# Attention scores as one plain fp32 product of q and k instead of three products of their split halves

## What is computed

```python
q = rms_norm((layernorm(x) @ Wq).reshape(b, lq, 4, 64), qn_w)
k, v = split(ctx @ Wkv);  k = rms_norm(k, kn_w)
attn = softmax(einsum('bqhd,bkhd->bhqk', q, k) / sqrt(64))
x = x + tanh(g_xattn) * (einsum('bhqk,bkhd->bqhd', attn, v) @ Wfc + fc_b)
xn = layernorm(x);  w, e = top2_softmax(xn @ Wr.T)
x = x + tanh(g_ffn) * sum_k w_k * (xn @ We[e_k])      # up to capacity 97
```

## Time and profile before

| | before |
|---|---|
| median of 3 runs | 1433.06 us |
| profiled execution | 1432.43 us |
| its span | 1430.7 us |
| TensorE, matmuls | 1396.8 us busy, 98% |
| TensorE, weight loads | 1174.7 us busy, 82% |
| VectorE | 77% busy |
| ScalarE | 65% busy |
| GpSimd | 54% busy |
| granted TensorE clock | 0.993 of full speed |

### The profile page before, as it was taken

The page is one execution under the profiler, slowest core; times in us unless marked ns, Lnnn a source line. Parts: engine busy times, 40 slices in busy tenths (PEclk is TensorE's granted clock), DMA queues, the critical chain, the costliest instruction groups (busy, mean ns, idle before and its releaser), DMA issues. The chain is left out here.

```text
span 1430.7 us, 27376 instructions
## 1 busy us (share of the span) xinstructions
PE 1396.8 (98%) x8478; PEld 1174.7 (82%) x8478; DVE 1108.2 (77%) x3146; ACT 926.7 (65%) x2600; POOL 768.8 (54%) x915
## 2 busy tenths in 40 slices
PE   5799999999999999999999999999999999999998
PEld 4688888888888888888888888888888888888876
DVE  6777878778878788878778878778778778777764
ACT  6656667666677666677666676666676666676652
POOL 3345555555555555555555555555554655554644
PEclk9899999999999999999999999999999999999999
DMA  5000000110100110100110100010101110101000
GB/s 150 20 9 28 34 35 9 35 35 28 35 19 24 35 35 27 35 15 29 35 35 28 35 9 35 35 35 28 35 9 35 35 35 28 35 9 35 16 16 23
DMA packets 29074, 43.65 MB, mean 31 GB/s; under 512 B 4672, under 2 KB 12288, under 8 KB 28928
## 3 DMA queue, kind: packets, MB, share of 16 engines
q1 hardware_dynamic: 28928, 41.90, 8.7%
HBM read 25.11 MB, written 16.78 MB: 29 GB/s over the span
## 5 line engine op out<-in xcount | busy, mean ns | idle before, releaser
L317 PE MATMUL bkM<-we,x2T 128*128 128x512 f32 x3072 | 784.7, 398 | 1.2 <-DVE acc_v L1029 1.2
L317 PEld LDWEIGHTS bkM<-we,x2T 128*128 128x128 f32 x3072 | 551.9, 188 | 125.3 <-ACT a_out L649 10.0
L649 ACT ACTIVATE a_out<-bkM,gate 128x256 f32<-128x256 f32 x512 | 215.6, 476 | 184.8 <-PE bkM L317 180.9
L1029 DVE SCALAR_TENSOR_TENSOR acc_v<-bkM,gate,acc_v 128x256 f32<-128x256 f32 x384 | 184.9, 481 | 48.0 <-PE bkM L317 32.9
L465 POOL TENSOR_TENSOR a_sum<-a_sum,a_out 128x256 f32<-128x256 f32 x256 | 188.5, 736 | 57.6 <-ACT a_out L649 21.1
L452 POOL TENSOR_TENSOR probs<-probs,p_inv 128x308 f32<-128x308 f32 x128 | 91.6, 717 | 177.1 <-DVE p_inv L922 177.1
L421 POOL TENSOR_TENSOR q_r<-q_ve,minus_half 128x16 f32<-128x16 f32 x32 | 93.1, 2911 | 112.8 <-DVE q_ve L907 112.8
L421 POOL TENSOR_TENSOR rstd<-ve,minus_half 128x4 f32<-128x4 f32 x64 | 65.3, 1020 | 159.6 <-DVE ve L822 159.4
L554 ACT ACTIVATE xn<-x_sb,shift,rstd 128x256 f32<-128x256 f32 x128 | 66.6, 590 | 94.2 <-DVE shift L831 94.2
L421 POOL TENSOR_TENSOR k_r<-k_ve,minus_half 77x8 f32<-77x8 f32 x32 | 52.3, 1636 | 130.7 <-DVE k_ve L871 130.7
L1029 DVE SCALAR_TENSOR_TENSOR acc_v<-bkM,gate,x 128x256 f32<-128x256 f32 x128 | 61.5, 481 | 64.0 <-PE bkM L317 62.2
(11 more groups left out here) (179 smaller groups left out, 2890.3 us busy)
## 6 DMA issues: line engine op xcount, KB each, us to landing
x_sb<-in_x SPq DMA_DIRECT2D x32, 512.0 KB, 3.8
out<-y SPq DMA_DIRECT2D x64, 256.0 KB, 2.0
ctx_sb<-in_ctx SPq DMA_DIRECT2D x32, 154.0 KB
stage<-in_L_ffn_We SPq DMA_DIRECT2D x2, 1024.0 KB, 6.3
stage<-in_L_xattn_Wkv SPq DMA_DIRECT2D x1, 512.0 KB, 6.2
stage<-in_L_xattn_Wq SPq DMA_DIRECT2D x1, 256.0 KB, 6.4
stage<-in_L_xattn_Wfc SPq DMA_DIRECT2D x1, 256.0 KB, 4.6
bias_bc<-in_L_xattn_fc_b SPq DMA_DIRECT2D x1, 128.0 KB, 5.5
```

What stands on the lines that cost most here:

```text
L317: mm = nc.tensor.matmul(out, l, r, start=(i == 0), stop=(i == len(terms) - 1))
L649: ins = nc.scalar.activation(a_out[:, t % 2, (e // 4) * 2 + i], bkM[1][:, i * D:(i + 1) * D], ACT.Copy, scale=gate[:, m.parity, t, e:e + 1])
L1029: nc.vector.scalar_tensor_tensor(out=acc_v[:, t], in0=bkM[0][:, i * D:(i + 1) * D], scalar=gate[:, m.parity, t, e:e + 1], in1=src, op0=ALU ...
```

## The change

The scores are multiplied from unsplit q and k in plain F32: one matmul for each m in place of three. ScalarE's copies now write plain F32 into `kd` and `qT`. VectorE no longer makes the low halves, so `k_part` and `q` are gone from its stream, and TensorE waits for ScalarE's copies themselves. Everything else keeps its place and order.

```diff
-        kd = sb("kd", [P, 2, BP, KC, 2, LK], F32R)
+        kd = sb("kd", [P, BP, KC, 2, LK])
-        qT = sb("qT", [P, 2, KC, TOK], F32R)
+        qT = sb("qT", [P, KC, TOK])
...
-                copy(qT[:, 0, :, i * LQ:(i + 1) * LQ], qT_half(f, i)).then_inc(q_hi.sem, 1)
+                copy(qT[:, :, i * LQ:(i + 1) * LQ], qT_half(f, i)).then_inc(qT_done.sem, 1)
...
-                    copy(kd[h, 0, :, :, j], kT_psum[h], scale=qk_w[h, 2:3]).then_inc(k_hi.sem, 1)
+                    copy(kd[h, :, :, j], kT_psum[h], scale=qk_w[h, 2:3]).then_inc(kd_done.sem, 1)
...
-            def k_part(f):
-                for j in range(2):
-                    dve.wait_ge(k_hi.sem, k_hi.at(f, j + 1))
-                    h = slice(j * DH, (j + 1) * DH)
-                    nc.vector.scalar_tensor_tensor(out=kd[h, 1, :, :, j], in0=kT_psum[h], scalar=qk_w[h, 2:3],
-                                                   in1=kd[h, 0, :, :, j].bitcast(F32), op0=ALU.mult,
-                                                   op1=ALU.subtract).then_inc(k_lo.sem, 1)
-
-            def q(f, i):
-                dve.wait_ge(q_hi.sem, q_hi.at(f, i + 1))
-                half = slice(i * LQ, (i + 1) * LQ)
-                lo(qT[:, 1, :, half], qT_half(f, i), qT[:, 0, :, half]).then_inc(q_lo.sem, 1)
...
-                    if f:
-                        k_part(f)
                 if k == 7 and f:
                     q_sums(f, 1)
                     q_mean(f)
-                    q(f, 0)
                 if k == 8:
-                    if f:
-                        q(f, 1)
                     chunk(k, m, p)
...
-                q(f, 0)
-                k_part(f)
-                q(f, 1)
                 weights_lo([FRONT_WEIGHTS + 1])
...
-                pe.wait_ge(k_lo.sem, k_lo.at(f))
-                pe.wait_ge(q_lo.sem, q_lo.at(f, 1 if t == 0 else SUB))
+                pe.wait_ge(kd_done.sem, kd_done.at(f))
+                pe.wait_ge(qT_done.sem, qT_done.at(f, 1 if t == 0 else SUB))
                 for m in range(KC):
-                    mm = product(s_bank[t][:, m * 2 * LK:(m + 1) * 2 * LK], [
-                        ([qT[:, a, m, t * P:(t + 1) * P] for a in range(2)],
-                         [kd[:, a, t // SUB, m].rearrange("p j k -> p (j k)") for a in range(2)])])
+                    mm = pe.matmul(s_bank[t][:, m * 2 * LK:(m + 1) * 2 * LK], qT[:, m, t * P:(t + 1) * P],
+                                   kd[:, t // SUB, m].rearrange("p j k -> p (j k)"), start=True, stop=True)
                 mm.then_inc(s_ps.sem, 1)
```

More of the change, by code:

```diff
@@ L226, in build @@
         kT_ps = sig("kT_ps", 1)
-        k_hi = sig("k_hi", 2)
-        k_lo = sig("k_lo", 2)
+        kd_done = sig("kd_done", 2)
         q_ps = sig("q_ps", SUB)
@@ L233, in build @@
         qT_ps = sig("qT_ps", SUB)
-        q_hi = sig("q_hi", SUB)
-        q_lo = sig("q_lo", SUB)
+        qT_done = sig("qT_done", SUB)
         q_ve_done = sig("q_ve_done", 1)
@@ L784, in _ @@
         def _(dve):
-            dve.memset(kd[:].bitcast(F32).rearrange("p a b c d e -> p (a b c d e)"), 0.0).then_inc(setup_v, 1)
+            dve.memset(kd[:].rearrange("p b c d e -> p (b c d e)"), 0.0).then_inc(setup_v, 1)
             dve.memset(vz[:].bitcast(F32).rearrange("p a b c d -> p (a b c d)"), 0.0).then_inc(setup_v, 1)
```

## The result

The changed kernel takes 1422.49 us (median of four runs, 1420.55 to 1424.39), the kernel before 1432.53 beside it (1431.90 to 1433.73): a ratio of 0.9933, with a 95% interval from 0.9921 to 0.9944. That is 10.0 us less, where 15.0 were forecast. The time lies in the stated range, but in no rival's own: between the 1421 at which A ends and the 1424 at which B begins. Timed again later it took 1421.74 us beside 1432.60, a ratio of 0.9928 (0.9916 to 0.9940). The profiled execution took 1423.5 us with a span of 1421.8, at a granted clock of 0.992.

A forecast was written before the change was run, and what follows sets the result against it. The stretch to attention was taken as bound by a VectorE, ScalarE, VectorE lane (13.75 us) over TensorE's work (13.42). 30 x 0.47 = 14.1 plus 0.9 in the fill, 15.0 us less, gave 1418.0 us; range 1412 to 1438.

The forecast's parts named there:

- A: The forecast itself: scores at most 0.635 us a tile, chain 0.47 us shorter; 1418 us, bounds 1415 to 1421; 58%.
- B: Chain not shortened: `eq` held by something else, or another operation hits GpSimd's additions; 1424 to 1432.5, about 1431 us; 18%.
- The cost of plain fp32: TensorE's scores: two plain products taken at 0.53 us a tile, against 0.67 for six matmuls; bounds 0.26 and 0.89.
- rival C: Slower: plain fp32 loads weights for each of four passes or can't hide loads; 0.89 us a tile, 1450 us; 20%.
- The clue of `eq`: VectorE's `eq`, 0.78 us, is held until GpSimd's `xb` additions end; an earlier sum of squares frees it 0.47 us sooner.
- such a collision: Another operation of VectorE's chain runs into GpSimd's additions at its new place, costing up to 0.6 us each.
- the bound which the prediction had put at 0.58: ScalarE isn't free for tile 1 before `a_out` is out of the way, so at most 0.58 us can be had.
- At 0.67, unchanged, 0.33 us a step are still gained: With TensorE's scores still 0.67 us a tile, VectorE's removed work alone still gains 0.33 us a step.
- the 0.47 of the sum: From first scores to attention, the VectorE, ScalarE, VectorE lane shortens 0.47 us in each of 30 steps: 14.1 us.
- TensorE's own work, 13.42: First scores to attention: TensorE's work takes 13.42 of 13.75 us, the other 0.33 being waits; 12.86 after the change.
- Behind attention nothing: Behind attention TensorE runs chunk upon chunk and nothing removed is waited for there: no gain or loss counted.
- The fill, -0.9: In the fill's first round, without the `qT` subtraction the shift of pair 1 comes earlier and ScalarE stops waiting: -0.9 us.

The follow-up runs named there:

- e10: On e4, GpSimd makes all four `xb` additions ahead of `q_r`: 1416.94 us, ratio 0.9890.
- e8: Kernel before, with VectorE's row maximum of tile 3 moved ahead of the chunk of slot 10: 1427.54 us, ratio 0.9967.
- e1: Kernel before, with VectorE's sum of squares and mean moved ahead of the `kd` subtractions, nothing removed: 1434.19 us, ratio 1.0009.
- e2: Kernel before without VectorE's four subtractions for the low halves, which stay zero; six matmuls a tile kept: 1432.57 us, ratio 0.9993.
- e9: Kernel before with the order changes of both e1 and e8, no work removed: 1420.12 us, ratio 0.9915.
- e4: Changed kernel plus two unused tiles beside `kd` and `qT`, so later tiles keep their old addresses: 1416.74 us, ratio 0.9888.
- e13: Kernel before plus 32 unused bytes per partition behind `kd`, nothing else changed: 1435.68 us, ratio 1.0019.
- e7: Changed kernel plus 32 unused bytes per partition behind `kd`, restoring only the offset within 64 bytes: 1420.27 us, ratio 0.9917.

## Why the prediction was right, and where it wasn't

**The cost of plain fp32: right.** Taken at 0.53 us a tile, measured 0.53 and 0.52. It is the last of the cases that the prediction listed, two streams at the transposes' pace: each product is two loads and two matmuls, 0.131 us / 154 = 0.85 ns a column each, against the transposes' 0.84. The prediction took 0.53 from between that case and four streams at 0.55, so the last hundredth is luck. The rule of the Trainium skill ("FP8 and Floating Point Precision", section TensorE Precision Notes), four passes for a true fp32 product, stood beside rival C (the prediction calls it the second) with 0.89 us a tile, each pass at the price of one of today's matmuls. The trace doesn't bear out that price: whatever the number of passes, which no run counts, the whole costs 0.525 / 0.67 = 0.78 of the three products, since those ran at 0.112 us each. Rival C falls with it.

**The clue of `eq`: right, with a new hold beside it.** The sum of squares starts 0.03 us after `q_sq` ends, 0.49 sooner than before, and `q_r` and `xb` follow. `eq` lost not 0.47 but 0.59 us, as it is no longer held at all. But `s_bias`, two instructions ahead of the routing, is now held for 0.18 us: it ends at 708.31, where the second of the three additions ends (706.86 + 2 x 0.71 = 708.28). The prediction had named such a collision as a possibility, and put it at nothing in the sum. The net is -0.41 for `egap` in place of -0.47. That is also the bound which the prediction had put at 0.58, less the hold: ScalarE has no idle time left between tile 0's exponentials and `egap`, and these begin 0.17 us later behind the first scores (708.34 - 706.35 = 1.99, before 711.92 - 710.10 = 1.82). e10, in which the additions are elsewhere, has `s_bias` at 0.16 and `eq` at 0.19, so the hold is theirs. Only instructions with two inputs in SBUF were held: `s_bias` reads `s_max` and `q_r`, `eq` reads `lg` and `top`, while the copies and maxima between them (`lg_lo`, `top`) last what they last without GpSimd. The Trainium skill, "SBUF — State Buffer", section Who interferes with whom, has this rule: a VectorE instruction with two inputs in SBUF contends with a GpSimd instruction that reads SBUF, and the ports that the two engines share are an exclusive lock. The trace agrees: the held ones end 0.03 and 0.05 us behind an addition. An `s_bias` or `eq` that starts 0.09 us before an addition's end lasts no longer than elsewhere (711.73 before, 708.89 after).

The same coincidence of ends stands in VectorE's lane, and behind the last reciprocal, in every kernel here; the prediction, which took `eq` for the one odd row, passed over it. In the kernel before:

```profile
718.00 0.70 POOL L452 TENSOR_TENSOR probs<-probs,p_inv 128x308 f32<-128x308 f32 x1 [1.78 <-DVE p_inv L922]
```

`gap` (718.03, 0.69 us) ends 0.02 us behind it. Likewise `w_top`, 0.49 us on 4 numbers a partition, ends 0.01 us behind the last work on `probs`, and `g_part`, 0.71 us on 32 numbers, 0.06 behind an addition for `a_sum`; both lie between the last reciprocal and attention. Operations of these sizes last 0.16 to 0.19 us elsewhere, so some 1.4 us of a step's stretch may be such waiting, an estimate from these rows (0.53 + 0.33 + 0.53). No run tried to take it away.

**Two lanes that meet at attention: the step that failed.** The prediction followed the chain back from `pT` to `egap` and to ScalarE, and took the stretch for ScalarE's lane against TensorE's own work. But the gates stand behind the last reciprocal in VectorE's stream, and that stands behind VectorE's own work since the chunk of slot 10, with 0.81 us of idle time before it that TensorE ended. This third lane reached the reciprocal at 10.52 where ScalarE's would have let it go at 10.14 + 0.20 = 10.34, and did in e8. It ruled, by 0.18 us. In the timeline of before ScalarE had no idle time after 714.80, and neither had VectorE after 716.25; I took the first for the chain and never asked what the second waited for.

Three sentences fall with it. "TensorE's saving doesn't show by itself, it only makes room": without it e1 and e2 gain nothing. "At 0.67, unchanged, 0.33 us a step are still gained": e2 is that case, and even the end of its interval gains 0.16% where that would have been 0.7%. And the 0.47 of the sum has no right to its good fit: attention moved by 0.53, as VectorE's lane did (10.52 to 9.99), while ScalarE's by itself would have allowed -0.38 (10.34 to 9.96). Attention starts 3.23 us after the later of the two in every kernel of the table but e9, where TensorE's own work is the longest.

**TensorE's own work, 13.42: right.** In e9 it is what is left, at 13.36. That TensorE's wait for `pT` would be as long as before or longer, not gone, was wrong. The waits of the loads from 75 to 1380 us (total, times, longest), to be held against the earlier trace rows:

```profile
PEld bkM L315 <- ACT a_out L647: 13.2, 30, 0.6
...
PEld bkF L315 <- issue: 7.3, 30, 0.3
```

The load for attention waits 6.1 us less, the load for a chunk 3.2 us more, as ScalarE's `a_out` is now late behind exponentials of its lane. By the starts TensorE still waits 13.22 - (13.42 - 4 x 0.145) = 0.38 us a step, all of it in the four chunks and none ahead of attention.

**Rival B** named the right place for a miss, "the chain is not shortened", with the wrong reason. VectorE's part of the change alone is B's result, 1432 to 1434 us; that it was not the result of the whole is TensorE's doing.

**"Behind attention nothing": wrong, and it is the missing 5 us.** 0.18 us a step were lost there, 29 x 0.18 = 5.2. The cost of the smaller tiles, that everything behind them moves, wasn't in the list of parts. With the old places (e4) the change gives 1432.5 x 0.9888 = 1416.5 us, 16 us in place of 10. 0.13 of the 0.18 are shown to come from the places. The last 0.05 stays open. It isn't peculiar to plain products: the rest of the step (period less attention) takes 29.38 us before and 29.43 in e4, but 29.42 in e8 too, which only exchanges lines of the kernel before.

**The fill, -0.9: neither shown nor refuted.** The first pair's scores start 1.7 us sooner (26.06, before 27.77), the third pair's 1.3 later in one profile and 0.3 sooner in the other. Over all kernels here the latter lies between 104.9 and 108.6. e1 has the largest; its exchange stands in `slot`, which the first round of the fill runs too, and 0.5 us were foreseen for it there. But e9 has the same exchange and 106.69, and e8, whose fill does what it did before, has its first scores at 26.34 and the third pair's at 105.72. An effect of one microsecond can't be read from single profiles of the fill.

That 0.47 stands so near to the measured 0.53 is luck: the lane that ruled happened to shorten by about as much as was forecast for the other. The sum as it should have been: 29 x 0.53 = 15.4 for the stretch, less 29 x 0.18 = 5.2 for the rest of the step, and a fill that is good for one or two microseconds either way: 10.2 us less, 1422.

## What to carry to other kernels

An engine that is "busy without a pause" back to some row isn't thereby the end of the search: of two chains that join, look at both up to the waits that open them, and price the difference between them, since cutting the longer one pays only that much and cutting the shorter one nothing. Here 0.18 us lay between them, and the arithmetic that was saved, 88 us of VectorE and 17 us of TensorE (4 x 0.145 in 30 steps), gained no more than an exchange of a few lines did. And when a change alters the size of a tile, its neighbours move: hold the old places once, to see what is the change and what is the shift.

## What the runs showed of the hardware

- A plain fp32 product of 128 x 128 stationary and 154 moving numbers appears as two weight loads and two matmuls, 0.262 us together, against 0.336 for three matmuls of split numbers.
- Where tiles lie in SBUF changes the pace of matmuls of 512 columns: 231 ns from start to start became 234, a median duration of 393 became 397, and 32 bytes alone cost 0.10 us a step (e13). How much of the effect is the offset within 64 bytes isn't settled: taking it away gave back 0.06 of 0.13 us a step (e7), adding it cost 0.10 (e13). Which operand matters and why was not tried.
- An operation on 4 numbers a partition can double in time (0.16 to 0.34 us), and one on 32 can take four times as long (0.19 to 0.78), through an addition on GpSimd that nothing in the program connects with it. With these additions elsewhere (e10) both last 0.16 and 0.19.
